# First attention of a two-layer kernel: the group norm's inverse square root as one power operation on GpSimd, and the decay's affine step on ScalarE

## The reference, cut to what matters

```
out = _wkv_scan(r, k, v, w)              # state * exp(w_t) + k_t v_t, read out with r_t
w   = -softplus(-proj(lerp(mix_w), w_w)) - 0.5
mu  = out.mean(axis=-1); var = out.var(axis=-1)       # over the 8 channels of a head
out = (out - mu) / sqrt(var + 0.00064)
out = out * gn_weight + gn_bias
return (out * g) @ out_w.T
```

## Time and profile before

| | us |
|---|---|
| median of three runs | 1323.47 |
| lowest and highest | 1320.85, 1325.7 |
| the profiled execution | 1323.05 |
| its span, first to last instruction | 1321.2 |
| GpSimd busy, whole span | 605.6 (46%) |
| VectorE busy | 820.8 (62%) |
| ScalarE busy | 497.1 (38%) |
| TensorE busy | 1157.1 (88%) |

### The profile page before, as it was taken

The page is one execution under the profiler, slowest core; times in us unless marked ns, Lnnn a source line. Parts: engine busy times, 40 slices in busy tenths (PEclk is TensorE's granted clock), DMA queues, the critical chain, the costliest instruction groups (busy, mean ns, idle before and its releaser), DMA issues.

```text
span 1321.2 us, 23979 instructions
## 1 busy us (share of the span) xinstructions
PE 1157.1 (88%) x8027; PEld 816.0 (62%) x8027; DVE 820.8 (62%) x2275; ACT 497.1 (38%) x1147; POOL 605.6 (46%) x706
## 2 busy tenths in 40 slices
PE   6868869867788889899999999999998899999990
PEld 3545546555358886346556465475554599999990
DVE  4678868887334444445457687766646366666665
ACT  3324434433314442142434444424331145444440
POOL 1556858887525554512224546532246233333330
PEclk9788989998889999998889999969899899999996
DMA  4976697673134522100101012000011341111106
GB/s 135 258 185 160 165 260 176 155 164 80 35 76 115 153 80 69 60 23 24 47 10 57 26 49 73 25 23 18 22 39 41 76 118 42 38 46 37 44 20 198
DMA packets 96530, 113.07 MB, mean 86 GB/s; under 512 B 11225, under 2 KB 81177, under 8 KB 93833
## 3 DMA queue, kind: packets, MB, share of 16 engines
q1 hardware_dynamic: 87512, 93.17, 27.1%
q0 software_dynamic: 8640, 17.84, 4.2%
q10 hardware_dynamic: 256, 0.53, 0.2%
HBM read 81.06 MB, written 32.04 MB: 86 GB/s over the span
## 4 chain that ended last, share of the span: by engine, by line
PE 58%; issue 11%; DVE 9%; DMA 8%; POOL 7%; ACT 3%; SPq 2%; DVEq 0%; ACTq 0%; POOLq 0%
PE bank L2027 8%; PE bank L2038 8%; PE bank L2247 5%; PE bank L2185 4%; PE bank L2137 4%; PE bank L2054 3%; PE bank L2194 3%; PE bank L2149 3%; PE bank L2224 3%; PE bank L2213 2%; POOL slots L1234 2%; DMA mrow<-mods 2%; DMA region<-vrdram 2%; POOL region L1270 2%; PE bank L2209 2%
## 5 line engine op out<-in xcount | busy, mean ns | idle before, releaser
L2027 PE MATMUL bank<-rows,wup 128*128 128x128 f32 x1136 | 154.7, 280 | 17.4 <-DVE wup L763 14.1
L1234 POOL DMA_INDIRECT slots<-pay,slot x128 | 130.0, 1016 | 83.4 <-issue 71.6
L1249 POOL DMA_INDIRECT y<-region,xin x78 | 83.9, 1075 | 154.0 <-ACT region L1614 140.7
L2027 PEld LDWEIGHTS bank<-rows,wup 128*128 128x128 f32 x1136 | 141.0, 195 | 21.3 <-DVE rows L751 10.4
L2038 PE MATMUL bank<-rows,wse 128*128 128x128 f32 x1136 | 141.9, 278 | 2.7 <-DVE wse L768 2.7
L2038 PEld LDWEIGHTS bank<-rows,wse 128*128 128x128 f32 x1136 | 132.2, 192 | 9.1 <-issue 7.9
L1036 DVE TENSOR_REDUCE rows<-bank 128x4 f32<-128x512 f32 x128 | 79.5, 684 | 92.6 <-PE bank L2137 86.7
L1249 POOL DMA_INDIRECT y<-hh,region x64 | 69.2, 1082 | 92.9 <-ACT hh L1614 81.9
L1702 ACT ACTIVATE w0uv<-bank 128x512 f32<-128x512 f32 x128 | 66.1, 602 | 90.5 <-PE bank L2194 90.4
L756 DVE SCALAR_TENSOR_TENSOR rows<-bank,bcol,rows 128x128 f32<-128x128 f32 x142 | 43.4, 346 | 90.8 <-ACT rows L1603 90.5
L1790 PE MATMUL bank<-consts 128*128 128x512 f32 x192 | 92.2, 627 | 0.0
(11 more groups left out here) (334 smaller groups left out, 2405.3 us busy)
## 6 DMA issues: line engine op xcount, KB each, us to landing
region<-vrdram SPq DMA_DIRECT2D x16, 1024.0 KB
region<-vrdram SPq DMA_DIRECT2D x32, 512.0 KB, 7.7
xin<-slots SPq DMA_DIRECT2D x78, 65.0 KB
region<-slots SPq DMA_DIRECT2D x64, 65.0 KB
wgl<-in_wgl SPq DMA_DIRECT2D x8, 512.0 KB
rows<-y SPq DMA_DIRECT2D x8, 512.0 KB, 4.3
wgl<-y SPq DMA_DIRECT2D x8, 512.0 KB, 6.5
xres<-x SPq DMA_DIRECT2D x12, 256.0 KB
```

The costliest lines, as they stand in the source:

```text
L1234: p.indirect_dma_start(io["slots"], bass.IndirectOffsetOnAxis(ap=slot_of(l, b)[:, k, t:t + 1], axis=0), pay_of(l, b)[:, k, t, :], None).th ...
L1249: p.indirect_dma_start(io["y"], bass.IndirectOffsetOnAxis(ap=xins[par][:, h, k, P + 1:P + 2].bitcast(U32), axis=0), bYs[par][:, h, k, :], ...
L2027: ins = M(bank_up(l, n)[:, tile(j)], wup[:, n % 3, tile(j)], bxT[:, q % 2, tile(k)], start=True, stop=True)
```

## The change

head_rsqrt on GpSimd becomes one operation: gnr's variance to the power -0.5, the exponent being one column of nhalf broadcast over 64. The first guess on VectorE (two integer operations) goes away, and the semaphore a_gn counts 3 per row in place of 16. GpSimd's decay goes away; ScalarE does the affine step itself, with a second activation on the tile that its tanh has just written, and waits for the tanh in between.

```diff
@@ VectorE
                 def link(ins):
                     n[0] += 1
                     ins.then_inc(S["a_gn"], 1)
-                    if n[0] < 4:
-                        v.wait_ge(S["a_gn"], b * 16 + n[0])
-                gv, gy = gnr[:, 0, :], gnr[:, 1, :]
+                    if n[0] < 2:
+                        v.wait_ge(S["a_gn"], b * 3 + n[0])
+                gv = gnr[:, 0, :]
                 v.wait_ge(S["a_sq"], 2 * b + 2)
                 link(V.tensor_reduce(gv, sq.rearrange("p (a c) -> p a c", c=DH), axis=AX, op=ALU.add))
                 link(V.tensor_scalar(gv, gv, 1.0 / DH, GN_EPS, ALU.mult, ALU.add))
-                link(V.tensor_scalar(gy.bitcast(I32), gv.bitcast(I32), 1, None, ALU.logical_shift_right))
-                link(V.tensor_scalar(gy.bitcast(I32), gy.bitcast(I32), -1.0, float(RSQRT_MAGIC), ALU.mult, ALU.add))
             def head_norm(b):
-                v.wait_ge(S["a_gn"], b * 16 + 16)
+                v.wait_ge(S["a_gn"], b * 3 + 3)
@@ GpSimd
-            def decay(a):
-                p.wait_ge(S["a_tz"], a + 1)
-                settled(p)
-                G_.tensor_scalar(decs[a % 2], decs[a % 2], 1.0, DECAY, ALU.add, ALU.mult).then_inc(S["a_dec"], 1)
             def head_rsqrt(b):
-                n = [4]
-                def link(ins):
-                    n[0] += 1
-                    ins.then_inc(S["a_gn"], 1)
-                    p.wait_ge(S["a_gn"], b * 16 + n[0])
-                gv, gy, ga_ = gnr[:, 0, :], gnr[:, 1, :], gnr[:, 2, :]
-                p.wait_ge(S["a_gn"], b * 16 + 4)
-                for _ in range(3):
-                    link(G_.tensor_tensor(ga_, gy, gy, ALU.mult))
-                    link(G_.tensor_tensor(ga_, ga_, gv, ALU.mult))
-                    link(G_.tensor_scalar(ga_, ga_, -0.5, 1.5, ALU.mult, ALU.add))
-                    link(G_.tensor_tensor(gy, gy, ga_, ALU.mult))
+                gv, gy = gnr[:, 0, :], gnr[:, 1, :]
+                p.wait_ge(S["a_gn"], b * 3 + 2)
+                G_.tensor_tensor(gy, gv, nhalf[:, 0:1].to_broadcast([P, 64]), ALU.pow).then_inc(S["a_gn"], 1)
@@ GpSimd, step
-                if ok(a):
-                    decay(a)
@@ ScalarE
                 A.activation(decs[b % 2], bank[2][:, :], ACT.Tanh, scale=0.5).then_inc(S["a_tz"], 1)
+                a.wait_ge(S["a_tz"], b + 1)
+                A.activation(decs[b % 2], decs[b % 2], ACT.Copy, scale=DECAY, bias=DECAY).then_inc(S["a_dec"], 1)
```

## The result

The changed kernel takes 1358.32 us in the median of four runs (1355.52 to 1362.3), the kernel before 1324.59 us in its four; the ratio is 1.0257, with a 95% interval of 1.0224 to 1.0291. It is slower. Medians are of all runs, ratios and intervals of the undisturbed ones, so a ratio need not be that of the medians. The forecast was 1365.6 us and slower with a chance of 0.62; the range, 1319 to 1368 us, holds the result. The profiled execution took 1355.52 us with a span of 1353.7 us, 32.5 us more than before.

The account below looks back on a forecast made before the run. The first attention's rows were taken as paced by the later of the gate row's load and GpSimd's own work. The power's added time less idle time summed to 42.5 us: 1323.05 + 42.5 = 1365.6 us, range 1319 to 1368.

Parts of the forecast that it names:

- The two clocks: Each first-attention row is paced by the later of the gate row's load and GpSimd's own work; load waits total 31.0 us.
- the upper end: GpSimd's 128 x 64 power, its extra cost over a multiply counted wholly per column: 13.76 us; the lower end was 1.13.
- rival B: Part of the power's price on GpSimd is paid once, so it is cheaper: 1323 to 1350 us, chance 0.27.
- The idle times: GpSimd's waits before gated_out in six of eight rows, 31.0 us in all, absorb added time first.
- E: Time added per row on GpSimd by the power replacing the Newton operations, forecast as +9.22 us.
- the forecast's own list: Idle time before gated_out by row, subtracted from the added time: 8.95, 7.73, 0.66, 9.18, 0, 1.35, 3.11, 0 us.
- the forecast's own case: GpSimd's power takes 11 to 13.8 us: 1350 to 1368 us, chance 0.45.
- I count no second wait: VectorE's head_norm and units 2 to 5, queued behind the power, catch up before GpSimd needs them: 0 us.
- the 8.5 us of the earlier trace: GpSimd reaches received(1) only 8.5 us after head_rsqrt's end, giving VectorE time to be ahead again.
- its move gains nothing, as forecast: Moving the decay off GpSimd, 0.71 us a row, goes into the indirect DMAs' slot wait: value 0.
- Rival C: Power mostly fixed-price, 1.13 us: gains 3.4 to 5.0 us, mainly in row eight; 1318 to 1319.7 us, chance 0.23.
- The sum of 42.5 us: Forecast loss over the first attention's eight rows, after idle time absorbs its part of 9.22 us a row.

Follow-up runs that it names:

- Experiment 3: Kernel before with one multiply of 128 x 64 in place of the twelve Newton operations: 1322.93 us against 1321.49, ratio 1.0028.
- experiment 7: Kernel before with residual and gate row loads issued earlier and one multiply replacing the Newton operations: 1299.08 us, ratio 0.9782.
- 5: Kernel before with the residual and gate row loads issued one group of the recurrence's rows earlier, Newton operations kept: 1318.26 us against 1331.22, ratio 0.9834.
- experiment 4: Kernel before with sixteen more chained multiplies behind the Newton operations, making head_rsqrt as long as with the power: 1352.83 us against 1321.49, ratio 1.0295.
- experiment 8: Kernel before with powers of 1 to 128 columns on scratch data behind GpSimd's other work: 0.159 us a column plus 0.43 us once.
- the repeated one: The changed kernel itself, run again on another chip: 1325.45 us against 1294.65 for the kernel before, ratio 1.0226.
- Experiments 9 and 10: Changed kernel with VectorE's units 2 and 3 before head_norm, ratio 1.0202; changed kernel with the next row's decay projection before the head transposes, 1324.67 us.
- experiment 1: Kernel before with the power in place of the Newton operations, decay left on GpSimd: 1350.42 us against 1321.49, ratio 1.0213.
- experiment 2: Kernel before with only the decay's affine step moved to ScalarE, Newton operations kept: 1325.03 us against 1321.49, ratio 1.0058.

## Why the prediction held, and what it had wrong

**What bounds: shown for the kernel before.** The two clocks are there. Experiment 3 took 4.2 us a row from GpSimd and gained nothing in the time and at most 2.4 us at row eight; with the loads earlier the same cut brought 11.2 us there (experiment 7 against 5); experiment 4 added 6 us a row and lost what the power loses. Two clocks are not the whole of it, though: of the 33.6 us cut in experiment 7 two thirds were not gained, and VectorE stands behind both clocks.

**The power's price: right kind, a quarter too high.** The forecast took the upper end, 13.76 us; it is 10.52. The step that failed is the split of the 0.842 us that the small power costs over a small multiply: "all of it per column". By experiment 8 it is 0.43 us once and 0.159 a column, while a whole multiply of 4 columns costs 0.2. That a part is paid once was rival B's reading. The rule of the Trainium skill, GPSIMD Engine Reference, Instruction dispatch, that the operation is a loop over the elements, agrees with the straight line; that all of the extra time then belongs to the loop, as the forecast read it, does not. The other figure of the Trainium skill, 2.6 cycles per element for a two-input operation (GPSIMD Engine Reference, Elementwise side-by-side cycle accounting), does not hold for a power: 0.159 us a column is, as an estimate by that page's 1.2 GHz, some 190 cycles.

**The idle times: right, and the range met partly by luck.** With the measured price E is 10.52 + 0.08 - 4.62 = 6.0 us, and the sum by the forecast's own list is 0 + 0 + 5.3 + 0 + 6.0 + 4.6 + 2.9 + 6.0 = 24.8 us. At gated_out of row eight it was 28.2 in the profiled execution and 27.7 in the repeated one. Rows five to eight grew by 5.8, 5.2, 3.3 and 5.5 us against 6.0, 4.6, 2.9 and 6.0. But a price of 10.52 us is under the 11 with which the forecast's own case began: it is rival B's, and its sum gives 1323.05 + 24.8 = 1347.9 us, in B's range of 1323 to 1350. That the execution took 1355.5 us, inside the forecast's 1350 to 1368, comes from row three and from the stages behind, 7.7 us that no case had. The direction, slower, did not need that luck.

**"I count no second wait": wrong in row three.** It grew by 9.6 us where 5.3 were due; row four gave 1.4 back. The timeline of GpSimd in the changed kernel names the waits:

```profile
116.63 1.27 POOL L1291 TENSOR_TENSOR rows<-rows,wgl 128x512 f32<-128x512 f32 x1 [1.00 <-ACT rows L1496]
126.80 0.23 POOL L1209 TENSOR_SCALAR veps<-mv 128x4 f32<-128x4 f32 x1 [2.08 <-DVE mv L619]
129.67 1.27 POOL L1263 TENSOR_TENSOR region<-region 128x512 f32<-128x512 f32 x1 [0.92 <-DVE region L917]
131.66 1.27 POOL L1263 TENSOR_TENSOR region<-region 128x512 f32<-128x512 f32 x1 [0.71 <-DVE pay L692]
136.05 1.21 POOL L1232 DMA_INDIRECT slots<-pay,slot  x1 [3.12 <-issue]
```

Of these, only the last was there before, with 1.91 us. In step 2 GpSimd has no indirect DMAs between head_rsqrt and gated_y, so the 8.5 us of the earlier trace rows on which the forecast relied are not there, and everything behind head_norm is late for it: y1, the statistics, the units. With sixteen multiplies in place of the power the row is nearly as long, 45.9 us, with 2.13 us for the statistics and 0.93 us for the scan, so this too comes from the length. Experiments 9 and 10 show two queues behind head_norm, each about as long; that no other thing lengthens the row is argued.

**The decay: its move gains nothing, as forecast; that it costs nothing is not shown.** Its 0.71 us went into the wait before the indirect DMAs (31.7 us against 26.5). Beside the power, with the decay on GpSimd (experiment 1) row eight stands at 363.81 us, with it on ScalarE at 366.07 and 365.50. With the Newton operations kept it is the other way round, 337.83 and 336.79 us. Both differences are of the size of the scatter, and the 0.2 to 1.0% of experiment 2 is not explained.

**Rival C's sum was too large.** It gave a cheap power 3.4 to 5.0 us. By experiment 3 a cut of 4.2 us a row gains nothing in the time (at most 1 us by the interval) and at most 2.4 us at row eight; the row without a bracket, five, had the load right behind.

The sum of 42.5 us against the measured 32.5 is then: 17.7 too much from the price, 3.4 too little from row three and the small differences of the others, and 4.3 too little behind the eight rows: 0.8 in the first attention's end and 3.5 in the later stages, which scatter by more.

## What to carry to other kernels

Count an operation by its columns before trading many cheap ones for it: two sizes of it on the chip give the fixed part and the part per column, and a replacement that wins on 4 columns (1.0 us against an estimated 3.5) can lose on 64 (10.5 against 4.6). A missing wait in front of one engine does not make it the bound; see what waits in the other rows, and take work away to find out. Where a load is the second clock, moving it earlier in its queue (here 1.2 to 1.7%) is worth more than making the engine beside it faster, and together they bring row eight's gated_out 27.5 us forward, where alone they bring 16.3 and at most 2.4.

## What was not expected of the hardware

A power on GpSimd costs 0.159 us a column of 128 x n plus 0.43 us, straight within 0.3 us from 1 to 128 columns, the same for all ones and for other numbers and for exponents from one column or a full tile; the multiply of 64 columns costs 0.32 us, 33 times less.

The second: VectorE's head_norm, 0.67 to 0.69 us in all eight rows before, took 1.74 us in rows two to seven of the changed kernel, where it was released by the power together with received(0) on GpSimd, which runs beside it. In row eight, where the power released it too but no received(0) follows, it took 0.69 us, and in row one, where it started later, 0.67. Which of the two starts first decides. Row three of the changed kernel, and of the kernel with sixteen multiplies in place of the power:

```profile
155.23 1.26 POOL L1263 TENSOR_TENSOR region<-region 128x512 f32<-128x512 f32 x1
155.30 1.74 DVE L939 TENSOR_TENSOR wgl<-wgl,gnr 128x512 f32<-128x512 f32 x1 [5.94 <-POOL gnr L1281]
...
153.47 0.69 DVE L941 TENSOR_TENSOR wgl<-wgl,gnr 128x512 f32<-128x512 f32 x1 [5.97 <-POOL gnr L1300]
153.52 1.78 POOL L1270 TENSOR_TENSOR region<-region 128x512 f32<-128x512 f32 x1
```

After the power, received(0) starts 0.07 us ahead, keeps its 1.26 us, and head_norm takes 1.74. After a chain of multiplies, head_norm starts 0.05 us ahead, keeps 0.69, and received(0) takes 1.78; so it was in rows three to five before. Either way both are done some 1.8 us after the first start, nearly the sum of 1.26 and 0.69: the one that comes second gets little done until the first has ended. In time it hardly matters here, since row eight of the two kernels stands within 0.6 us. What they contend for is not shown by these runs.
